# Four stages in one unrolled block: projection and tail run in pieces between the key tiles of the attention

## What is computed

```python
S = einsum('bhnd,bhmd->bhnm', Q, K) / dh**0.5      # 16 heads of 8; 1024 x 1024 scores each
W_tau = softmax(S)
W_sigma = 1 / ((1 + |S| / beta)**2 + t**2);  W_sigma /= W_sigma.sum(-1)
f = 0.5 * W_tau @ V + 0.5 * W_sigma @ V
y = f @ Wo.T + bo
x1 = x + (LN(x) + ln_w * LN(y) + ln_b)             # layer 1
w = softmax(LN(x1) @ gate_w + gate_b); w = w * (w >= 0.1); w /= sum(w)
x2 = x1 + sum_e w[e] * (LN(x1) @ expert_w[e] + expert_b[e])         # 8 experts of 128 x 128
x3 = x2 + causal_attention(LN(x2))                 # one head of 64
g = sigmoid((LN(x3) @ Wq.T) @ routers.T)           # 255 nodes of a binary tree of depth 8
x4 = x3 + ((product of g or 1-g along each path) @ leaf_values) @ Wout.T + bout
```

## Time and profile before

| | us |
|---|---|
| median of 3 runs | 2238.96 (2237.18 to 2242.65) |
| the profiled execution, time | 2231.01 |
| the profiled execution, span | 2229.2 |
| granted PE clock, mean | 0.886 of 2.4 GHz |

### The profile page before, as it was taken

How to read it: one execution, slowest core, us unless ns; L and a number is a source line. 1 busy time by engine, 2 the same in 40 slices (tenths; PEclk the granted TensorE clock), 3 DMA queues, 4 the chain that set the end, 5 groups by cost and what they waited for, 6 DMA issues and landing times. The chain is left out here.

```text
span 2229.2 us, 34812 instructions
## 1 busy us (share of the span) xinstructions
PE 1688.8 (76%) x8579; PEld 605.2 (27%) x8579; DVE 1744.0 (78%) x3634; ACT 1737.8 (78%) x1716; POOL 1365.5 (61%) x1198
## 2 busy tenths in 40 slices
PE   5477777777777777777777777777777757889876
PEld 2222122222212222222222212222222234456655
DVE  6788888888888887888888888888888458854556
ACT  3389999999999999999999999999999911122243
POOL 2387877777787787777777777777777412000000
PEclk8699999988999998999999999999899977877778
DMA  3300000000000000000000000000000000000001
GB/s 103 95 6 12 11 14 13 11 11 11 11 11 12 15 11 11 11 11 11 11 14 13 11 11 11 11 11 12 14 11 11 1 0 0 0 1 0 0 1 38
DMA packets 28862, 31.74 MB, mean 14 GB/s; under 512 B 5209, under 2 KB 16544, under 8 KB 28832
## 3 DMA queue, kind: packets, MB, share of 16 engines
q1 hardware_dynamic: 28832, 31.40, 4.7%
HBM read 22.74 MB, written 8.39 MB: 14 GB/s over the span
## 5 line engine op out<-in xcount | busy, mean ns | idle before, releaser
L702 DVE TENSOR_SCALAR sigma_weights<-ps_sig 128x512 int32<-128x512 int32 x1024 | 694.2, 678 | 233.2 <-PE ps_sig L609 230.2
L848 POOL TENSOR_TENSOR sigma_weights<-grown 128x832 f32<-128x832 f32 x512 | 805.4, 1573 | 0.0
L596 PE MATMUL ps_acc<-tau_weights,v_operand 128*9 128x512 f32 x2048 | 577.7, 645 | 290.2 <-ACT sums L784 150.4
L824 POOL TENSOR_SCALAR grown<-sigma_weights,shape_operand 128x832 f32<-128x832 f32 x512 | 491.1, 959 | 367.4 <-DVE sigma_weights L702 360.0
L709 DVE TENSOR_TENSOR running_max<-ps_sig,running_max 128x512 f32<-128x512 f32 x896 | 608.4, 679 | 0.0
L799 ACT ACTIVATE tau_weights<-ps_tau 128x1024 f32<-128x1024 f32 x512 | 514.5, 1005 | 83.3 <-PE ps_tau L627 82.7
L596 PE MATMUL ps_acc<-sigma_weights,v_operand 128*9 128x512 f32 x2048 | 579.1, 646 | 0.1
L756 ACT ACTIVATE sigma_weights<-sigma_weights,shape_operand 128x2048 f32<-128x2048 f32 x256 | 509.9, 1992 | 5.9 <-POOL sigma_weights L848 5.9
L609 PE MATMUL ps_sig<-q_operand,k_operand 96*128 96x512 bf16 x1024 | 421.7, 412 | 110.8 <-DVE running_max L709 93.8
L762 ACT ACTIVATE sigma_weights<-sigma_weights 128x2048 f32<-128x2048 f32 x256 | 485.5, 1896 | 0.1
L627 PE MATMUL ps_tau<-q_operand,k_operand 128*128 128x512 bf16 x1024 | 328.7, 404 | 0.2 <-DMA q_operand<-max_rows 0.2
(11 more groups left out here) (172 smaller groups left out, 1496.4 us busy)
## 6 DMA issues: line engine op xcount, KB each, us to landing
q_operand<-q_parts SPq DMA_DIRECT2D x192, 48.0 KB
k_operand<-k_parts SPq DMA_DIRECT2D x64, 144.0 KB
q_parts<-parts SPq DMA_DIRECT2D x12, 256.0 KB, 2.9
k_parts<-parts SPq DMA_DIRECT2D x12, 256.0 KB, 2.9
x_res<-in_L_attn_x SPq DMA_DIRECT2D x4, 512.0 KB, 7.0
q_operand<-max_rows SPq DMA_DIRECT2D x128, 2.0 KB
out<-x_res SPq DMA_DIRECT2D x4, 512.0 KB, 3.2
experts<-in_L_ffn_expert_w SPq DMA_DIRECT2D x1, 512.0 KB
```

The source lines that it names most:

```text
L596: mm = pe.matmul(ps_acc[32 * q:32 * q + COLS, :], vop[:, (slot - 1 + kind) % SLOTS, j, :], weights[:, half * HALF:(half + 1) * HALF], star ...
L702: dve.tensor_scalar(sig[:, tile % SIG_RING, cols].bitcast(I32), ps_sig[:, half, :].bitcast(I32), SIGN_OFF, None, ALU.bitwise_and)\
L824: pool.tensor_scalar(grown[:, tile % GROWN_RING, :], u, 1.0, shape[:, slot, 0:1], ALU.mult, ALU.add)\
L848: pool.tensor_tensor(sig[:, tile % SIG_RING, ACT_COLS:N], t, t, ALU.mult)\
```

## The change

The six blocks become one block, with no loop: every instruction of all 512 tiles is written out. Each engine walks over slots g = 0 to 533, one key tile a slot, and between the fixed instructions of a slot it calls `beside.upto(x)`, which emits the side pieces that are due by x. A side piece is a few instructions of another stage; its due time is a number written by hand. Projection of batch b+1 is due in slots 0 to 21 of batch b, the tail (everything behind the attention) of batch b-1 in slots 22 to 127 of batch b. Only projection 0 stands ahead of slot 0, and only tail 3 behind slot 533.

- All side matmuls use two PSUM banks in turn (`ps_side`, numbered by `USE`): a matmul into a bank waits until the use two before has been read (`take`, `side_read`). The banks come from `ps_tau`, which now has one slot of two banks: the scores of tile g wait for the exponential of tile g-1.
- POOL takes the whole square, 1024 columns; ACT's part is gone. ACT's copies of the sums and of the maximum row go to DVE (L1058, L1051). The sums of a head are divided in PSUM.
- Lags: weighing 9 tiles behind, shifted scores 13. The operands of head n are issued three slots ahead of it.
- The tail is computed another way: biases come in through matmuls of three bf16 rows; the output norm uses centred weights; the causal scores are made a second time, transposed, and exponentiated straight into the operand of the weighing, so nothing is transposed there; the tree takes logarithms (|logit|/2, then exp and ln) and one matmul with a path matrix (L635, L641) and an exponential in place of the levels. Everything stays in one ACT table set.
- In batch 0, in place of a tail, `prepare` builds the folded weights and the path matrices, the latter with some 50 POOL instructions of 256 columns (L1433 to L1455).

The diff, cut to its core:

```diff
-        load_weights(nc, a, w)
-        project_heads(nc, a, w)
-        attend_heads(nc, a, w)
-        mix_experts(nc, w)
-        attend_causal(nc, w)
-        descend_tree(nc, w, out)
-        ps_tau = ps("ps_tau", [P, 2, 2, HALF])
+        ps_tau, ps_sig = ps("ps_tau", [P, 2, HALF]), ps("ps_sig", [P, 2, HALF])
+        ps_misc, ps_acc = ps("ps_misc", [P, HALF]), ps("ps_acc", [P, HALF])
+        ps_side = [ps(f"ps_side{i}", [P, HALF]) for i in range(2)]
+class Beside:
+    def upto(self, slot):
+        while self.due <= slot:
+            self.due = next(self.pieces, float("inf"))
...
+            def take(n):                                   # PE, ahead of a side matmul
+                wait(pe, side_read[n % 2], n // 2)
+                for i in range(2 * TB):                    # PE: experts
+                    n, t, half = u(f"e{i}"), i // 2, i % 2
+                    yield t0 + (20.5 + 0.5 * i if i < 2 else 24 + 1.5 * (i - 1))
+                    take(n)
+                    biased(n, 0, HALF, ROW_E + half * HALF)
+                    done(pe.matmul(bank(n)[:, :], zt[:, t * P:(t + 1) * P], experts[:, 4 * half:4 * half + 4, :],
+                                   start=False, stop=True), n)
...
+                def arrive(i):                             # PE: tree
+                    take(n)
+                    pe.matmul(bank(n)[:, :], leaf_router[:, of], zt[:, g * HALF:(g + 1) * HALF], start=True, stop=False)
+                    for q in range(2):
+                        pe.matmul(bank(n)[:, :], path[:, q, of], sizes[:, 2 * g + q, :], start=False, stop=False)
+                def arrive_logs(i):
+                    for q in range(2):
+                        mm = pe.matmul(bank(n)[:, :], path[:, q, of], logs[:, 2 * g + q, :], start=False, stop=q == 1)
...
+            def tau_scores(g):
+                wait(pe, tau_done, g)
...
+            for g in range(SLOTS_ALL):                     # PE
+                    sigma_scores(g, 0)
+                    turn_running(head, 0)                  # first slot of a head
+                beside.upto(g)
+                    tau_scores(g - TAU_LAG)
+                beside.upto(g + 0.25)
+                    sigma_scores(g, 1)
+                beside.upto(g + 0.5)
+                    weigh(g - PV_LAG)
+                beside.upto(g + 0.75)
...
+                for i in range(2 * TB):                    # DVE: experts
+                    for q in range(4):
+                        yield t0 + 24.25 + 1.5 * i + 0.37 * q
+                        ins = dve.scalar_tensor_tensor(out=xt(b, t), in0=bank(n)[:, q * D:(q + 1) * D], scalar=weight[:, t, e:e + 1],
+                                                       in1=xt(b, t), op0=ALU.mult, op1=ALU.add)
...
+            for g in range(SLOTS_ALL):                     # DVE
+                    take_sums((g - SUMS_AT) // TB)
+                    magnitude(g, 0)
+                beside.upto(g)
+                    maximum(g, 0)
+                beside.upto(g + 0.25)
+                    magnitude(g, 1)
+                beside.upto(g + 0.5)
+                    maximum(g, 1)
+                beside.upto(g + 0.75)
...
+            for g in range(SLOTS_ALL):                     # ACT
+                    tau_weights(g - TAU_LAG)
+                beside.upto(g)
+                    invert((g - EXP_LAG) // CHUNK)         # every second slot
+                    take_logs((g - LOG_LAG) // CHUNK)      # the other slots
+                beside.upto(g + 0.5)
...
-                act.activation(tile, tile, ACT.Square, bias=shape[:, slot, 0:1]).then_inc(sqa_ready, 1)
-                u = sig[:, tile % SIG_RING, ACT_COLS:N]
+                pool.tensor_scalar(grown[:, g % GROWN_RING, :], sig[:, g % SIG_RING, :], 1.0, shape[:, g // TB % H, 0:1],
+                                   ALU.mult, ALU.add).then_inc(grown_ready, 1)
+                pool.tensor_tensor(sig[:, g % SIG_RING, :], t, t, ALU.mult).then_inc(sq_ready, 1)
```

2336 lines of the change are left out of this document (1184 added, 1152 removed).

## The result

Five executions of each kernel in turn on one chip: 2261.14 us (2253.58 to 2278.43) after the change, 2238.96 (2231.55 to 2242.65) before. The ratio is 1.0112 with a 95% interval of 1.0065 to 1.0159: 1.1% slower. I had said 2130 and at most 2225. The profiled execution took 2263.25 us with a span of 2261.5.

A forecast was written before the change was run, and what follows sets the result against it. ACT bounds the attention now, with 441 us of tail stages behind it; after the change POOL is first at 3.00 us a slot. Start 40, attention 1887, drain 38 and last tail 155 make a 2120 span, median 2130; range 2010 to 2225.

The forecast's parts named there:

- the price of the waits beside a tail: Batches 1 to 3 of the attention: 104 of 200 us of side work exposed, 488 us a batch, 475 without projection.
- the experts' interlock: Slots 46 to 71: expert matmuls wait for an earlier addition; 4.2 us a slot, 105 us against DVE's 88.
- the projection and the slots behind it: Slots 0 to 7: 22 us; 7 to 22, POOL-bound with two short bank waits: 60; 22 to 34, ACT-bound: 41.
- norm stretches and weighing: Second norm and gate 31 us, two free slots 6; slots 71 to 81, 39; weights and weighing, slots 95 to 110, 58.
- the tree and the slots behind it: Slots 116 to 124: PE-bound, 37.5 us, 40 with waits; the last four slots of the batch 12 us.
- Slots without a tail: Batch 0, slots 54 to 127: about 3.08 us a slot, POOL over 95% busy; batch 0 in all 436 us.
- The port: About eight DVE side instructions a batch, reading two SBUF tiles, wait for POOL: 0.5 us each, 4 us.
- late operands: Rival: each head's operands 4 us late, 64 heads pay 256 us, time 2380; included in a chance of 0.1.
- PE's slot: PE's own loop work in one slot of the attention, estimated by starts at 2.05 us.
- Behind the loop: Drain and last tail after the last scores: drain 38 us, last tail run alone about 155 (135 to 190).
- point of no gain: Attention of 1996 us, 520 a batch, 136 of 200 us side work exposed; chance of more than two thirds 0.1.
- a chain through `ps_tau`: Slower rival: side pieces of PE, DVE and ACT add up through its single slot; fully exposed 2420 us; chance 0.1.

The follow-up runs named there:

- the two due times moved: Changed kernel with expert matmuls 0.75 slot later and the projection's second half 2 slots later, its store behind the operands' load: 2133.89 us, ratio 0.9527 to the kernel before.

## Why the prediction was wrong, step by step

The step that failed is the price of the waits beside a tail. Of the 46 us that batch 2 is over its forecast of 488, the experts' interlock, named and priced too low, holds 14; the projection and the slots behind it, with a wait for stored parts that was priced at nothing, 9; norm stretches and weighing 18; the tree and the slots behind it 9; slots 81 to 95 give 4 back.

- **Slots without a tail: right.** Batch 0 took 441 (436), its slots 54 to 127 3.2 each (3.08), POOL 94% busy in them (221.92 of 236.5; over 95% forecast). The sum for batch 0 counts 129 slots in place of 128, 3 us too much. ACT's and PE's coupling through the one slot of `ps_tau` did no harm in them.
- **The port: right, and small.** I added 4 us a batch for eight DVE instructions, shifts and gate, that wait for POOL, by the nearest row. In batch 2 the four shifts (L794) took 0.55, 0.25, 0.97 and 0.46 us, where the last one, with POOL idle, took 0.17; of the gate's, L948 took 0.84 and alone 0.22, L934 and L941 0.52 and 0.43 and alone 0.22 and 0.17, and one, L931, was not longer. That is 2.7 us in sum. That it is POOL they wait for is read from the two cases, beside a busy POOL and beside an idle one. The loop's own L1085 shows none of it (groups by form between 22 and 2064 us, then over the whole run):

```profile
L794 DVE SCALAR_TENSOR_TENSOR shift<-mean_var,rstd 128x8 f32<-128x8 f32 x12 | 7.1, 590 | 0.4 <-ACT rstd L1153 0.4
L948 DVE TENSOR_TENSOR gate_weight<-gate_kept,gate_inverse 128x64 f32<-128x64 f32 x3 | 2.5, 841 | 0.0
```

```profile
L1085 DVE TENSOR_TENSOR f_tokens<-ps_misc,f_tokens 128x64 f32<-128x64 f32 x64 | 13.7, 214 | 0.1
```

  L1085 took the place of L688 and reads one input from PSUM: 214 ns in place of 851. The Trainium skill (SBUF — State Buffer, section "Who interferes with whom") says that a DVE instruction with at most one SBUF input doesn't contend with GpSimd; this row agrees.
- **The experts: the step that failed first.** The chain was right, link by link, and its size wrong: 4.2 a slot forecast, 4.76 measured, and 31.5 us above DVE's own time instead of 17. The prediction speaks of three us lost in three slots, but its 105 holds only 2.0 (17 us in 25 slots); 3.8 were lost. The bound is sound: without the wait 86.6 remain (88 forecast). 14 of the 46 us that batch 2 is over are here, and in the end this one wait was 32 us a batch, about 91 in the time, four times what the change lost in all (22). One link was priced at the fast clock alone: bias and matmul, 1.08 in the prediction, take 1.28 from start to start in all 14 cases once the due times are moved by 0.25 or 0.75 slot, and in the changed kernel 2.2 to 2.5 in five of 14 (1238.09 to 1240.62 is one), 6 us more in the stretch.
- **The projection and what stands behind it: not seen.** I priced "two short bank waits of PE" and took 82 and 41 for slots 0 to 34. The wait of ACT for the stored parts isn't in my list of waits that the change adds, though `high` holds it. It costs 10 to 16 us a projection with the late operands, 34 in the time. The same wait stands in the start: ACT's parts of the second half of batch 0 wait for the stores of the first. In the timeline of the start, first ACT and then PE:

```profile
28.81 0.69 ACT L1189 ACTIVATE parts<-ps_side,bq_col 128x512 bf16<-128x512 f32 x1 [7.17 <-DMA k_parts<-parts]
```

```profile
46.68 1.01 PE L680 MATMUL ps_sig<-q_operand,k_operand 96*128 96x512 bf16 x2 [12.93 <-DMA k_operand<-k_parts]
```

  The scores start at 46.7, where the earlier trace rows has 96.50, inside my 36 to 48, and 6.7 later than forecast; ACT stood 7.17 us there. No run takes that wait away.
- **PE's slot: nearly right where PE bounds; the slots behind the tree were not priced.** I took 2.05 a slot from starts. Over batch 2 the loop's own instructions come to 2.44 (313 us by the distances of their starts), but that mean holds stretches at the slow clock. In the tree's eight slots, at a granted clock of 1.00, they come to 17.1 us, 2.1 a slot, and the tail's to 21.2: 38.3, where I had 15.6 and 21.9, that is 37.5. The stretch took 42.4 in place of 40. The larger part of the 61.2 in place of 52 lies in slots 124 to 128, to which I gave 3.0 each, 12 in all, and which took 18.8. The leaf matmuls stand in PE's order there, first behind a wait for ACT's exponential, then for 4.4 us of their own:

```profile
1547.28 0.21 PE L415 MATMUL ps_side<-bias_rows,ones 3*128 3x128 bf16 x1 [2.20 <-ACT side_big L1341]
```

- **Norm stretches and weighing: 18 us too little.** Slots 34 to 46, 71 to 81 and 95 to 110 were 151.7 in place of 134. No engine is over 88% busy there. In slots 95 to 110 PE was busy 55.5 us where I had 51. The waits of PE for ACT that I find are small (2.3 us for the normalised rows in 34 to 46, 2.9 for the exponentials in 95 to 110). Copies on DVE took 2 to 4 us off slots 71 to 81 of each batch, later transposes 1 to 2; what the rest is stays open.
- **One stretch was better than forecast.** Slots 81 to 95 took 44.8 in place of 48.5, though PE was 95% busy in slots 81 to 91 (33.0 of 34.7).
- **Behind the loop: right.** 197.5 us for 193.
- **Chances.** My point of no gain was a batch of 520, that is 136 of 200 us of side work exposed, and had a chance of 0.1. With batch 3 shorter by 13, as in the rest of the sum, it is 524. Batch 2 took 534, 150 exposed. I had argued that only a chain through `ps_tau` or late operands could do that, and the chains that the runs found were others, but for operands 5 us late once a projection. I gave each of several places its likeliest price, and any place not thought of was priced at nothing; nearly all errors then went one way.
- **What would have been luck.** With the two due times moved, the batches (435, 491, 485 and 478) and the time (2134) stand within 4 us of my 436, 488, 488, 475 and 2130. That isn't the prediction come true: the experts are 17 us under their 105 there, and the norms, the weighing and the last slots make up for it.
